# Relative attention: shifts spread in bf16, and packed heads read in three transfers instead of six

## The reference

```
qk   = einsum('bhqd,bhkd->bhqk', qh, kh)
q_rk = einsum('bhqd,qkd->bhqk', qh, r_k)      # r_k = rk_table[clip(k - q) + P]
attn = softmax((qk + q_rk) / sqrt(d), axis=-1)
w1   = einsum('bhqk,bhkd->bhqd', attn, vh)
w2   = einsum('bhqk,qkd->bhqd', attn, r_v)
x    = x + tanh(g) * ((w1 + w2) @ Wo.T + bo)
```

## Time and profile before

| | us |
|---|---|
| median of 3 runs | 2859.22 (2847.67 to 2864.48) |
| the profiled execution, its own time | 2855.38 |
| its span (first to last instruction) | 2853.6 |
| PE busy | 2079.6 (73%) |
| DVE busy | 1270.3 (45%) |
| ACT busy | 839.7 (29%) |
| POOL busy | 560.0 (20%) |
| mean granted TensorE clock | 0.800 |

### The profile page before, as it was taken

One profiled execution on the slowest core, in us unless ns is written; L12 is line 12 of the kernel. 1 busy time (PEld: TensorE's weight loads), 2 busy tenths in 40 slices (PEclk: granted clock), 3 DMA queues, 4 the chain that ended last, 5 costly groups with the idle time before them and its releaser, 6 DMA issues. The chain is left out here.

```text
span 2853.6 us, 62464 instructions
## 1 busy us (share of the span) xinstructions
PE 2079.6 (73%) x25348; PEld 1616.3 (57%) x25348; DVE 1270.3 (45%) x2402; ACT 839.7 (29%) x1484; POOL 560.0 (20%) x523
## 2 busy tenths in 40 slices
PE   4777777773775497979797988887847766766663
PEld 3454445543664376767676767676735544544442
DVE  3444444445773254545454545454516662111112
ACT  2333333321222132423232424242314551111110
POOL 1111111110001010101010101010010005888881
PEclk8888988986887577978787878787867778888895
DMA  4445454431223212222222222222011214556556
GB/s 98 84 84 91 92 96 92 87 64 58 66 67 121 55 50 39 68 46 59 45 61 43 61 45 61 46 61 46 15 43 49 73 51 119 123 119 131 130 114 186
DMA packets 255381, 216.84 MB, mean 76 GB/s; under 512 B 70100, under 2 KB 234430, under 8 KB 255024
## 3 DMA queue, kind: packets, MB, share of 16 engines
q1 hardware_dynamic: 221008, 178.48, 27.0%
q0 software_dynamic: 24576, 27.05, 5.6%
q10 hardware_dynamic: 9568, 7.87, 0.9%
HBM read 147.08 MB, written 72.45 MB: 77 GB/s over the span
## 5 line engine op out<-in xcount | busy, mean ns | idle before, releaser
L1394 PE MATMUL r_ps_s<-r_q,r_rk 96*128 96x32 bf16 x4096 | 266.1, 237 | 83.6 <-DMA r_q<-parts_scratch 67.7
L1394 PEld LDWEIGHTS r_ps_s<-r_q,r_rk 96*128 96x128 bf16 x4096 | 249.0, 123 | 102.8 <-issue 82.9
L1165 DVE TENSOR_TENSOR r_score<-r_score,r_ps_t 128x1024 f32<-128x1024 f32 x128 | 155.5, 1218 | 207.6 <-PE r_ps_t L1405 207.5
L1270 ACT ACTIVATE r_score<-r_ps_s 128x512 f32<-128x512 f32 x256 | 152.9, 597 | 252.4 <-PE r_ps_s L1394 251.8
L1186 DVE TENSOR_TENSOR r_score<-r_ps_s,r_score 128x512 f32<-128x512 f32 x256 | 162.8, 684 | 100.5 <-PE r_ps_s L1425 99.5
L1471 PE MATMUL r_ps_b<-r_score,r_rv 128*32 128x32 f32 x8192 | 181.3, 261 | 11.0 <-issue 10.4
L1471 PEld LDWEIGHTS r_ps_b<-r_score,r_rv 128*32 128x32 f32 x8192 | 153.7, 134 | 36.3 <-issue 36.1
L1947 DVE TENSOR_TENSOR e_hT<-e_sil,e_ps_gu 128x256 f32<-128x256 f32 x64 | 27.0, 421 | 324.4 <-ACT e_sil L1969 228.9
L1425 PE MATMUL r_ps_s<-r_q,r_k 96*128 96x128 bf16 x1024 | 103.9, 241 | 74.2 <-DMA r_k<-parts_scratch 48.9
L313 DVE TENSOR_REDUCE a_row_max<-a_ps_s 128x2 f32<-128x512 f32 (+1 forms) x192 | 127.4, 686 | 62.0 <-PE a_ps_s L478 56.6
L1908 POOL DMA_INDIRECT e_rows<-rows_w_scratch,k_token x128 | 135.4, 1058 | 98.8 <-DVE e_h_last L1935 60.0
(11 more groups left out here) (293 smaller groups left out, 4323.7 us busy)
## 6 DMA issues: line engine op xcount, KB each, us to landing
a_q<-parts_scratch SPq DMA_DIRECT2D x96, 128.0 KB, 4.3
a_k<-parts_scratch SPq DMA_DIRECT2D x96, 128.0 KB, 4.2
r_q<-parts_scratch SPq DMA_DIRECT2D x48, 256.0 KB, 4.1
r_k<-parts_scratch SPq DMA_DIRECT2D x48, 256.0 KB, 4.2
e_wg<-in_L_ffn_expert_wg SPq DMA_DIRECT2D x64, 128.0 KB
e_wu<-in_L_ffn_expert_wu SPq DMA_DIRECT2D x64, 128.0 KB
e_wd<-in_L_ffn_expert_wd SPq DMA_DIRECT2D x64, 128.0 KB
rows_w_scratch<-m_row SPq DMA_DIRECT2D x8, 640.0 KB, 3.2
```

Of the source, the lines that this page charges most:

```text
L1165: dve.tensor_tensor(part, part, bcast(ps_t[m % 2][:], NT), ALU.add).then_inc(shifted, 1)
L1270: act.activation(score[1 - t][:, c // 8, :, q0:q0 + 16], ps_s[c % 2][:].rearrange("p (h q) -> p h q", h=BH), ACT.Copy).then_inc(place_copi ...
L1394: ins = pe.matmul(ps_s[c % 2][:].rearrange("p (h q) -> p q h", h=BH)[:, n, :], rk6[:, j:j + P], q6[:, :, q], start=True, stop=True)
```

## The change

Three things, all in `relative_attention`:

1. The scratch layout becomes (part, d, element, e, head, token), so that a partition's data is one run of 16 KB. `pack_parts` now issues two transfers of 64 KB for each part, one for each e.
2. The groups are ordered anew, with equal query parts side by side and key parts in an order that follows the layout: queries 0,0,0,1,1,2 and keys 0,1,2,0,1,0. Each side is read in three transfers: 48, 32 and 16 partitions. The source of a query read is one part, repeated by an outermost dimension of 3 or 2 with step 0; the source of a key read is 3, 2 or 1 parts that follow each other, taken as 48, 32 or 16 rows. Two key reads go ahead of the `w2` transfers, the last behind them.
3. The shift is kept as two bf16 terms, hi in partitions 0 to 31 and the rest in 32 to 63, for which PE writes the transposed maxima twice and DVE does a second operation; the spreading matmul is bf16 with 64 rows (`pick_row`, two identities on top of each other) in place of fp32r with 32.

```diff
+    Q_PARTS, K_PARTS = (0, 0, 0, 1, 1, 2), (0, 1, 2, 0, 1, 0)
+    READS = ((0, 3), (3, 2), (5, 1))
+    NR = len(READS)
...
-        ident, ident_r = sb("ident", [P, P], F32), sb("ident_r", [BH, BH], F32R)
+        ident, pick_row = sb("ident", [P, P], F32), sb("pick_row", [2 * BH, BH], BF16)
...
-        row_max, shift = sb("row_max", [P, BH], F32), sb("shift", [BH, P], F32R)
+        row_max, shift = sb("row_max", [P, BH], F32), sb("shift", [2 * BH, P], BF16)
...
+        pack_i = pack.rearrange("(i s) n e t -> i (s n e t)", s=NS).rearrange("i (n d s e h t) -> i n d s e h t", n=6, d=DH, s=NS,
+                                                                              e=ND, h=HE)
+        packed_rows = pack_i.rearrange("i n d s e h t -> i n d (s e h t)")
...
-                    sp.dma_start(pack_i[i, 3 * k + n, s].rearrange("(e p) t -> p e t", p=P), (q_parts, k_parts)[k][n][:])\
-                        .then_inc(packed_out, 16)
+                    for e in range(ND):
+                        sp.dma_start(pack_i[i, 3 * k + n, :, s, e], (q_parts, k_parts)[k][n][:, e, :]).then_inc(packed_out, 16)
...
-                for n, part in enumerate(Q_PARTS):
-                    sp.wait_ge(packed_q, START + 96 * i + 16 * n)
-                    sp.dma_start(heads_of(q6[n * DH:(n + 1) * DH]), rows_of(pack_i[i, part])).then_inc(packed_q, 16)
+                for r, (n, many) in enumerate(READS):
+                    sp.wait_ge(packed_q, START + 16 * NR * i + 16 * r)
+                    src = packed_rows[i, Q_PARTS[n]].unsqueeze(0).to_broadcast([many, DH, BH * S])
+                    sp.dma_start(q6[n * DH:(n + many) * DH].rearrange("p h t -> p (h t)"), src).then_inc(packed_q, 16)
...
-                for n in which:
-                    sp.wait_ge(packed_k, START + 96 * i + 16 * n)
-                    sp.dma_start(heads_of(k6[n * DH:(n + 1) * DH]), rows_of(pack_i[i, 3 + K_PARTS[n]])).then_inc(packed_k, 16)
-
-            FIRST_KEYS, LAST_KEYS = range(0, 3), range(3, len(K_PARTS))
+                for r in which:
+                    n, many = READS[r]
+                    sp.wait_ge(packed_k, START + 16 * NR * i + 16 * r)
+                    src = packed_rows[i, 3 + K_PARTS[n]:3 + K_PARTS[n] + many].rearrange("n d w -> (n d) w")
+                    sp.dma_start(k6[n * DH:(n + many) * DH].rearrange("p h t -> p (h t)"), src).then_inc(packed_k, 16)
+
+            FIRST_KEYS, LAST_KEYS = range(0, 2), range(2, NR)
...
-                    dve.tensor_scalar(shift[:], ps_t[0][0:BH, 0:P], -1.0, None, ALU.mult).then_inc(shift_ready, 1)
+                    dve.tensor_scalar(shift[:], ps_t[0][0:2 * BH, 0:P], -1.0, None, ALU.mult).then_inc(shift_ready, 1)
+                    dve.wait_ge(shift_ready, START + 2 * h + 3)
+                    dve.scalar_tensor_tensor(shift[BH:], ps_t[0][BH:2 * BH, 0:P], -1.0, shift[BH:], ALU.mult, ALU.subtract)\
+                        .then_inc(shift_ready, 1)
...
-                                            ident_r[:, 4 * m + n:4 * m + n + 1].to_broadcast([BH, P]),
+                                            pick_row[:, 4 * m + n:4 * m + n + 1].to_broadcast([2 * BH, P]),
                                             shift[:], start=True, stop=True)
...
-                    pe.transpose(ps_t[0][0:BH, 0:P], row_max[:], ident[:]).then_inc(max_turned, 1)
+                    pe.transpose(ps_t[0][0:BH, 0:P], row_max[:], ident[:])
+                    pe.matmul(ps_t[0][BH:2 * BH, 0:P], row_max[:], ident[:], start=True, stop=True, tile_position=(0, BH))\
+                        .then_inc(max_turned, 1)
```

More of the change, by code:

```diff
@@ L908, in relative_attention @@
         by_head = lambda a: a.rearrange("p t (e d h) -> p t e h d", e=ND, d=DH)
-        rows_of = lambda part: part.rearrange("s (e d h) t -> d s e (h t)", e=ND, d=DH)
-        heads_of = lambda a: a.rearrange("d (s e h) t -> d s e (h t)", s=NS, e=ND)
-        pack_i = pack.rearrange("(i s) n e t -> i (s n e t)", s=NS).rearrange("i (n s e t) -> i n s e t", n=6, s=NS, e=D)
+        pack_i = pack.rearrange("(i s) n e t -> i (s n e t)", s=NS).rearrange("i (n d s e h t) -> i n d s e h t", n=6, d=DH, s=NS,
+                                                                              e=ND, h=HE)
+        packed_rows = pack_i.rearrange("i n d s e h t -> i n d (s e h t)")
         def run(eng, step):
@@ L950, in pack_parts @@
                     sp.wait_ge(done, START + i * 8 + s * 4 + 2 * k + 2)
-                    sp.dma_start(pack_i[i, 3 * k + n, s].rearrange("(e p) t -> p e t", p=P), (q_parts, k_parts)[k][n][:])\
-                        .then_inc(packed_out, 16)
+                    for e in range(ND):
+                        sp.dma_start(pack_i[i, 3 * k + n, :, s, e], (q_parts, k_parts)[k][n][:, e, :]).then_inc(packed_out, 16)
             def take_queries(i, first=False):
-                sp.wait_ge(packed_out, START + i * 192 + 192)
+                sp.wait_ge(packed_out, START + i * 384 + 384)
                 if not first:
                     sp.wait_ge(scored, START + i * (2 * CH))
-                for n, part in enumerate(Q_PARTS):
-                    sp.wait_ge(packed_q, START + 96 * i + 16 * n)
-                    sp.dma_start(heads_of(q6[n * DH:(n + 1) * DH]), rows_of(pack_i[i, part])).then_inc(packed_q, 16)
+                for r, (n, many) in enumerate(READS):
+                    sp.wait_ge(packed_q, START + 16 * NR * i + 16 * r)
+                    src = packed_rows[i, Q_PARTS[n]].unsqueeze(0).to_broadcast([many, DH, BH * S])
+                    sp.dma_start(q6[n * DH:(n + many) * DH].rearrange("p h t -> p (h t)"), src).then_inc(packed_q, 16)
             def take_keys(i, which):
-                for n in which:
-                    sp.wait_ge(packed_k, START + 96 * i + 16 * n)
-                    sp.dma_start(heads_of(k6[n * DH:(n + 1) * DH]), rows_of(pack_i[i, 3 + K_PARTS[n]])).then_inc(packed_k, 16)
-            FIRST_KEYS, LAST_KEYS = range(0, 3), range(3, len(K_PARTS))
+                for r in which:
[4 more added lines that the diff above has]
+            FIRST_KEYS, LAST_KEYS = range(0, 2), range(2, NR)
             sp.dma_start(ctx_in[:], c_rows[0, 0]).then_inc(ctx_loaded, 16)
@@ L1093, in _ @@
             dve.wait_ge(const_made, START + 4)
-            dve.tensor_copy(ident_r[:], ident[0:BH, 0:BH]).then_inc(folded, 1)
-            dve.wait_ge(folded, START + 9)
-            dve.sem_inc(folded, 1)
+            for n in range(2):
+                rows = slice(n * BH, (n + 1) * BH)
+                dve.tensor_copy(pick_row[rows, :], ident[rows, rows]).then_inc(folded, 1)
             def normalise(i, s):
@@ L1239, in project @@
                     if n == 0:
-                        act.wait_ge(packed_out, START + i * 192 + s * 96)
+                        act.wait_ge(packed_out, START + i * 384 + s * 192)
                     act.activation(hi[:, n % 2, :], ps_proj[f % 2][:, 0:S], ACT.Identity,
@@ L1385, in step @@
                         if c == 0 and t == 1:
-                            pe.wait_ge(packed_q, START + 96 * (i + 1) + 96)
+                            pe.wait_ge(packed_q, START + 16 * NR * (i + 1) + 16 * NR)
                         if c == 0:
@@ L1400, in step @@
                         if m == 0:
-                            pe.wait_ge(shift_ready, START + h + 1)
+                            pe.wait_ge(shift_ready, START + 2 * h + 2)
                         if m >= 2:
@@ L1418, in step @@
                         if c == 0 and t == 1:
-                            pe.wait_ge(packed_k, START + 96 * (i + 1) + 96)
+                            pe.wait_ge(packed_k, START + 16 * NR * (i + 1) + 16 * NR)
                         if c < 2:
```

## The result

The changed kernel is slower: 2881.48 us median (2874.69 to 2886.69) against 2860.72 for the kernel before (2847.67 to 2864.48), a ratio of 1.0078 with a 95% interval from 1.0058 to 1.0098. Forecast were 2794 us and 83 in 100 for faster.

A forecast was written before the change was run, and what follows sets the result against it. PE was taken to bound relative attention, with waits for query and key reads. Odd steps 36.4 + even-step spreading 24.8 + first pair 0.9 - 0.4 = 61.7 us off the profiled 2855.4 gave 2794 us; range 2690 to 2840.

The forecast's parts named there:

- X: Time of a query read carried by few engines, 256 KB each: 13.0 us; the gain is zero at 16.9.
- Few engines: Query reads: the repeat of 3 or 2 confines them to 3 or 2 DMA engines, share near 0.19.
- Rival 1: Query reads: the repeat doesn't confine them and all 16 engines work; 155 us gained, 2700 us; 17 in 100.
- The rate: Confined query reads: each engine moves 23.3 GB/s, as a busy engine does in the large load.
- T0: The moment PE ends P2 of an even step; only then may SP overwrite the query buffer `q6`.
- the sum: Relative attention: odd steps 36.4, even steps 24.8, first pair 0.9, less 0.4; 61.7 us gained, 2794 us.
- Rival 2: Query reads: few engines at 12.9 GB/s, X = 22.1, query wait above 18 us; 2939 us; 13 in 100.
- The key read: Key reads in odd steps: 48 partitions on all engines take 5.5 us, and the key wait is gone.
- The odd steps: From T0, P2 starts at 49.8 us for 55.0: 5.2 us gained, seven times, 36.4.
- The writes: Scratch writes: six more issues per element, last key part out 2.3 us later; cost zero, 3.1 us of cover.
- The first pair: First pair of batch elements: P2 starts 45.4 us after the first query issue, before 46.3; 0.9 us gained.
- The spreading: P1: four bf16 spreads take 0.48 us for 1.04 at low clock; even steps gain 24.8 us, odd P1 19.4.

The follow-up runs named there:

- q_six: The changed kernel with six query reads of 16 partitions each, keys staying at three reads; 2776.70 us, ratio 0.9720 to the kernel before.
- port_order: The changed kernel with the group order turned round, so the 48-partition reads land in partitions 48 to 95; 2798.09 us, ratio 0.9797 to the kernel before.
- spread_only: The kernel before with only the bf16 spreads added, its layout, writes and reads unchanged; 2834.05 us, ratio 0.9919 to the kernel before.

## Why the prediction was wrong

The step that failed is **X for the 48-partition query read**. The text put every engine at 23.3 GB/s, took 13.0 us for both confined reads, and named 16.9 as the point from which the change loses, as one X for both. Measured were 21.6 and 12.3, a mean of 16.95, just at that point, and 7.9 us more than 26.0 for the two together; keys and writes then made a loss of it. The large load from which the rate came wrote all partitions; a read into 48 starting at 0 doesn't spread its three engines alike. Point by point:

- **Few engines (right).** Shares of 0.21 to 0.10 during the reads; q_six, without the confinement, is some 100 us faster than the changed kernel. Rival 1 falls; by it the time would have been 2700.
- **The rate (wrong by where the data lands).** A packet of 16 KB takes 0.61 us on one of the three engines and about 1.2 us on the other two. In port_order, with nothing changed but the partitions, X is 12.8 and 12.7, P1 starts 30.0 us after T0 (forecast 30.4), the key wait is 1.3 us in all, and the time is 2798 against a forecast of 2794. That is the kernel that the sum described. Rival 2 had the direction but not the mechanism: its engines were all to be slow, at 12.9 GB/s, with X = 22.1 for both reads and 2939 us. Its sign, a query wait of more than 18 us, did come, at 20.7, but from one slow read and not from two.
- **The key read.** Forecast 5.5 us for 48 partitions, on 16 engines; it took 9.3. So the key wait did not vanish: up to 2.2 us in each odd step, though every key read came later.
- **The odd steps.** From T0 to P2: forecast 49.8, measured 60.4 in the step shown (1262.31 - 1201.92) and 59.5 to 60.7 in all seven: 7.8 from the queries, 0.5 from P1 (19.9, not 19.4), 2.2 from the keys. Seven times 10.6 is 74 us.
- **The writes.** "Cost zero" was wrong in the first pair. Two issues take 1.28 us and follow each other at 1.47 for a part, against 0.75. In the loop the last one is out at 1197.42 + 1.28 = 1198.7 and lands some 2.1 us later, 1.1 us ahead of T0, not 3.1. In the first pair nothing covers them: from the first write of the second element to the first query issue it is 932.96 - 923.88 = 9.1 us, against 928.93 - 922.72 = 6.2 before, 2.9 us. That part was costed in the loop only.
- **The first pair.** P2 starts 53.9 us after the first query issue (forecast 45.4, before 46.3). With the writes this is a loss of 10.5 instead of a gain of 0.9, 11.4 us.
- **The spreading (right).** Four spreads in 0.54 us (forecast 0.48), and spread_only gives 21.6 us where 24.8 were forecast for the even steps. P1 of odd steps stayed at clock 0.50. The extra matmul and DVE operation cost nothing that shows.

The two corrections, 74 and 11.4, take 2794 to 2879; the profiled execution took 2874.7. The range, 2690 to 2840, failed with the same step: its upper end came from rates common to all engines, so it had no case in which one read is slow and the other isn't.

## What to carry to other kernels

Merging transfers saves waits only if the merged one has as many engines and as many ways into SBUF as the small ones: look at the outermost count of both sides and at the partitions it lands in, and price each transfer of another shape by itself. Here a repeat of 3 at the front left 3 engines, and moving the 48-partition reads of queries and keys up by 48 partitions was worth 80 us. A wait between transfers isn't always waste: with the reads in flight together PE stood still for 40 to 106 us in P3, so count its "issue" gaps before and after taking such waits away.

## What the runs showed of the hardware that was not expected

- The rate of a confined read depends on its destination: 58 and then 33 GB/s for three engines into partitions 0 to 47, 79 GB/s for three into 48 to 95. Into 0 to 47 two of the three took about 1.2 us for a packet of 16 KB and one 0.61; into 48 to 95 all three took 0.61.
- The same holds for 16 engines: 768 KB land in 9.3 us in partitions 0 to 47, in 6.9 in 48 to 95.
- With the DMA engines full (102% by the data queue), the instruction queue gets one packet in 16 us, and PE stands still for up to 10.6 us among matmuls that wait for nothing. It goes on 1.3 to 1.9 us after an instruction packet has ended.
- Two reads confined to 3 and to 2 engines take as long in flight together as one by one (29.7 and 30.0 us from T0 to P1), and once they are alone three packets are in flight at a time and then two, so that both use the same engines.
